# Attention 1 of a one-core vision tower: QKV from unnormalised rows, score row 7 summed on TensorE, a third value buffer for GpSimd, and an order of the value stage written out by hand

## The reference, cut to what matters

```
h = h + _L1_attn_ref(_layernorm(h, axis=-1), L1_attn_Wqkv, L1_attn_Wout)
h = h + _L1_ffn_ref(_layernorm(h, axis=-1), L1_ffn_base_W, ...)

def _layernorm(x, axis=-1, eps=1e-05):
    m = mean(x);  v = var(x);  return (x - m) / sqrt(v + eps)

def _L1_attn_ref(x, Wqkv, Wout):           # 16 heads of 16 channels, causal over the tiles
    q, k, v = split(x @ Wqkv.T)
    scores = clip(q . k / sqrt(16), -10, 10) + causal mask
    return (softmax(scores) @ v) @ Wout.T
```

## Time and profile before

| | us |
|---|---|
| median of 3 runs | 787.02 (785.82 to 787.16) |
| the profiled execution | 790.46 |
| its span in the trace | 788.6 |
| PE busy over the span | 701.5 |
| DVE busy | 499.5 |
| ACT busy | 391.7 |
| POOL busy | 420.2 |

### The profile page before, as it was taken

One profiled execution on the slowest core, in us unless ns is written; L12 is line 12 of the kernel. 1 busy time (PEld: TensorE's weight loads), 2 busy tenths in 40 slices (PEclk: granted clock), 3 DMA queues, 4 the chain that ended last, 5 costly groups with the idle time before them and its releaser, 6 DMA issues.

```text
span 788.6 us, 13036 instructions
## 1 busy us (share of the span) xinstructions
PE 701.5 (89%) x4209; PEld 600.4 (76%) x4209; DVE 499.5 (63%) x1182; ACT 391.7 (50%) x998; POOL 420.2 (53%) x358
## 2 busy tenths in 40 slices
PE   3999999999999999999829718999999999778788
PEld 3889998988989887654628618999999999435776
DVE  3678887777877787769989661322322232388966
ACT  4576675766757565533134433444444444147261
POOL 5767867768586760458869022334333432126860
PEclk9999999999999999999869957999999999779799
DMA  7955233432443030000030069899989993210001
GB/s 227 264 145 166 65 115 111 118 112 64 117 113 101 20 108 1 1 0 1 0 108 0 1 271 341 309 338 315 335 315 344 320 316 126 74 75 0 1 2 66
DMA packets 47085, 108.58 MB, mean 138 GB/s; under 512 B 5049, under 2 KB 24749, under 8 KB 39597
## 3 DMA queue, kind: packets, MB, share of 16 engines
q1 hardware_dynamic: 44428, 100.68, 38.4%
q0 software_dynamic: 2592, 7.10, 2.5%
HBM read 101.58 MB, written 6.17 MB: 137 GB/s over the span
## 4 chain that ended last, share of the span: by engine, by line
PE 72%; DVE 13%; POOL 4%; SPq 4%; ACT 3%; DMA 2%; issue 2%; DVEq 0%; ACTq 0%; POOLq 0%
PE banks L1808 12%; PE banks L1816 12%; PE banks L292 9%; PE banks L294 8%; PE banks L293 8%; PE banks L299 5%; PE banks L305 4%; PE banks L1348 3%; DVE a_o L1694 2%; DVE a_prod L1226 2%; SPq L386 2%; PE banks L1322 1%; PE banks L2159 1%; PE banks L1382 1%; POOL a_prod L1201 1%
## 5 line engine op out<-in xcount | busy, mean ns | idle before, releaser
L420 POOL TENSOR_TENSOR x_lo<-xraw,x_hi 128x512 fp32r<-128x512 f32 x81 | 106.3, 1312 | 77.8 <-ACT x_hi L414 77.7
L1898 ACT ACTIVATE hid<-banks,b 128x128 f32<-128x128 f32 x216 | 79.3, 367 | 110.4 <-PE banks L1808 107.8
L292 PE MATMUL banks<-wc_hi,x_hi 128*128 128x256 f32 x324 | 97.1, 300 | 13.3 <-POOL x_hi L423 9.8
L2065 DVE TENSOR_TENSOR res<-banks,xb 128x256 f32<-128x256 f32 x27 | 11.5, 424 | 127.9 <-PE banks L1816 127.9
L294 PE MATMUL banks<-wc_hi,x_lo 128*128 128x256 f32 x324 | 92.1, 284 | 0.0
L293 PE MATMUL banks<-wc_lo,x_hi 128*128 128x256 f32 x324 | 92.0, 284 | 0.0
L1936 POOL TENSOR_TENSOR y<-bve,mhalf 128x1 f32<-128x1 f32 x27 | 20.4, 755 | 105.6 <-DVE bve L2073 105.6
L456 DVE BATCH_NORM_STATS2 stats<-banks 128x6 f32<-128x256 f32 x81 | 34.6, 427 | 65.0 <-ACT pe_sb L450 64.3
L292 PEld LDWEIGHTS banks<-wc_hi,x_hi 128*128 128x128 f32 x324 | 62.1, 192 | 15.6 <-issue 10.0
L1808 PEld LDWEIGHTS banks<-xT,w_raw 128*128 128x128 f32 x448 | 68.0, 196 | 5.8 <-ACT xT L1886 0.9
L414 ACT ACTIVATE x_hi<-xraw 128x768 fp32r<-128x768 f32 (+1 forms) x81 | 66.6, 830 | 10.2 <-DMA xraw<-in_x_rest 10.2
(11 more groups left out here) (342 smaller groups left out, 1845.4 us busy)
## 6 DMA issues: line engine op xcount, KB each, us to landing
w_raw<-in_w SPq DMA_DIRECT2D x28, 1024.0 KB
xraw<-in_x_main SPq DMA_DIRECT2D x26, 768.0 KB
w1more<-in_w SPq DMA_DIRECT2D x13, 1024.0 KB
w2more<-in_w SPq DMA_DIRECT2D x13, 1024.0 KB
xraw<-in_x_rest SPq DMA_DIRECT2D x48, 96.0 KB
xraw<-in_x_rest SPq DMA_DIRECT2D x26, 114.0 KB
yl<-y_rows SPq DMA_DIRECT2D x2, 1028.0 KB, 6.9
a_w<-in_qkv_w SPq DMA_DIRECT2D x2, 768.0 KB, 5.4
```

The source lines that it names most:

```text
L292: pe.matmul(dst, a[0], b[0], start=start, stop=False)
L420: pool.tensor_tensor(x_lo[:, i % RING_X, :], xraw[:, k, 0:KF].rearrange("p c b -> p (c b)"), x_hi[:, i % RING_X, 0:KF * P], ALU.subtract). ...
L1898: act.activation(hid[:, s % 2, fc, :], bank(fc % 2, 0, P), ACT.Gelu, bias=b1[:, bass.ds(e * FC + fc, 1)]).then_inc(sem("gelu_made"), 1)
```

## The change

Six things change, all in attention 1 and around it.

1. The rows are not normalised before QKV. While the first experts' rows are gathered, PE sums the columns of `a_w[1]` with four matmuls against a matrix of ones, and DVE takes the column means off the weights (`center_qkv`, four operations). PE turns h itself, as soon as the pair of tiles is combined. The inverse deviation is applied when ACT copies q, k and v out of PSUM (`copy_scaled_qkv`). The ten normalisations on ACT and the three shifts on DVE go. Of rows that DVE reads as queries in PSUM (4, 6, 9) ACT scales the query in place, one more operation each.
2. Score rows: POOL makes the products of rows 1, 3, 5, 7, 8 (9 before, now DVE's). PE sums the products of row 7 by 16 matmuls; DVE only clips them. The first half of the softmax stands before DVE's last rows.
3. POOL has three slots for value products instead of two (the third is the buffer `yl`), and folds from four keys on instead of six, so rows 3 and 4 are folded too.
4. The order of PE and ACT in the value stage is written out call by call. The output products wait for all scores from row 0 on, not from row 2 on.
5. ACT measures rows 0 to 4 with two operations each (the mean comes out of the first one); DVE measures 5 to 9, and adds rows 7 and 8 to h before it waits for ACT's measurements.
6. The groups of z use the banks 2, 2, 3 instead of 2, 3, 2.

```diff
-        ON_ACT = 7
+        ON_ACT = 5
@@
-            jobs = [("row", t + 1, t == 6 if layer == 0 else t % 2 == 1)]
+            jobs = [("row", t + 1, t == 6 if layer == 0 else t in POOL_ROWS)]
...
+        POOL_ROWS = (1, 3, 5, 7, 8)
+        SUMMED_ROWS = {7: 6}
@@ def kept_keys
-            return (n + 1) // 2 if n > HALF else n
+            return (n + 1) // 2 if n > (HALF if layer == 0 else 3) else n
@@ def pool_slot
-            return a_prod[:, 2 + POOL_VALUES[layer].index(t) % 2, :]
+            i = POOL_VALUES[layer].index(t)
+            if layer == 1 and i % 3 == 2:
+                return yl[:, :, :].rearrange("p q c -> p (q c)")[:, 0:T * C]
+            return a_prod[:, 2 + i % (2 + layer), :]
@@
+        def pe_sum_row(pe, t):
+
+            n, i = t + 1, [job[0] for job in pool_jobs(1)].index(t)
+            pe.wait_ge(sem("a_pool_prod_made"), len(pool_jobs(0)) + i + 1)
+            by_channel = job_slot(1, i)[:, 0:n * C].rearrange("p (x d) -> p x d", d=D16)
+            for ch in range(D16):
+                last = pe.matmul(bank(SUMMED_ROWS[t], 0, n * H16), ident[:, :], by_channel[:, :, ch],
+                                 start=(ch == 0), stop=(ch == D16 - 1))
+            last.then_inc(sem("a_summed"), 1)
@@ def turn_x
-            pe.wait_ge(sem("a_xn_made"), seen(layer, "xn_made", t + 1))
+            if layer == 0:
+                pe.wait_ge(sem("a_xn_made"), t + 1)
+            else:
+                pe.wait_ge(sem("y_added"), 4 * (t // 2 + 1))
...
-            turn(pe, bank(t % 2), a_xn[:, t % 2, :]).then_inc(sem("a_turned"), 1)
+            turn(pe, bank(t % 2), a_xn[:, t % 2, :] if layer == 0 else h_at(t)).then_inc(sem("a_turned"), 1)
@@ def project_o
-                if layer == 1 and t == 2:
+                if layer == 1 and t == 0:
                     pe.wait_ge(sem("a_s_made"), seen(1, "s_made", T))
@@
+        def copy_scaled_qkv(act, t):
+            inverse = rstd[0][:, t:t + 1]
+            for part in range(3):
+                if t == batch_of("attention 1", part)[1]:
+                    act.wait_ge(sem("rstd_made"), batch_of("attention 1", part)[0] + 1)
+            act.wait_ge(sem("a_qkv_done"), seen(1, "qkv_done", 2 * t + 1))
+            a = 0
+            if t in queries_in_bank(1):
+                act.activation(qk_bank(t, 0, C), qk_bank(t, 0, C), ACT.Identity, scale=inverse)
+                a = C
+            act.activation(a_qkv[:, t, a:2 * C], qk_bank(t, a, 2 * C), ACT.Identity, scale=inverse).then_inc(sem("a_qkv_made"), 1)
...
@@ def dve_attention
-                for t in range(T + 1):
-                    if t < T:
-                        row_scores(dve, link, 1, t)
-                    if t == T - 2:
-                        softmax_half(dve, link, 1, 0)
+                for t in range(0, 8, 2):
+                    row_scores(dve, link, 1, t)
                     if t:
                         pool_sums(dve, link, 1, t - 1)
+                softmax_half(dve, link, 1, 0)
+                row_scores(dve, link, 1, T - 1)
+                pool_sums(dve, link, 1, T - 2)
...
+                    clip(dve, link, 1, "row", t, t + 1)
                 softmax_half(dve, link, 1, 1)
@@ end of the value stage on DVE
+                add_rows(dve, 8)
+                row_variances(dve, 2 * T + 2 * ON_ACT, ON_ACT)
                 for t in range(ON_ACT, T):
-                    add_rows(dve, t)
-                    dve.wait_ge(sem("a_h_made"), seen(1, "h_made", t + 1))
+                    if t == 7:
+                        add_rows(dve, 9)
+                    dve.wait_ge(sem("a_h_made"), seen(1, "h_made", T if t >= 7 else 9))
                     tile_stats(dve, "low rank", t, h_at(t))
-                    if t == ON_ACT:
-                        row_variances(dve, 2 * T + 3 * ON_ACT, ON_ACT)
...
-        ADDED = {5: ((0, 1), (2,)), 7: ((3,), (4,)), 9: ((5,), (6,))}
+        ADDED = {5: ((0, 1), (2,)), 7: ((3,), (4,)), 9: ((5,), (6, 7))}
@@
+        def center_qkv(dve):
+
+            dve.wait_ge(sem("route_summed"), 3)
+            for c in range(CH):
+                for means, a, b in ((bank(3, 0, 2 * C), 0, 2 * C), (bank(5), 2 * C, QKV)):
+                    dve.scalar_tensor_tensor(out=a_w[1][:, c, a:b], in0=means, scalar=-1.0 / C, in1=a_w[1][:, c, a:b],
+                                             op0=ALU.mult, op1=ALU.add)
```

149 lines of the change are left out of this document (93 added, 56 removed).

## The result

The changed kernel takes **780.6 us** (median of 4 runs, 778.46 to 781.80) against 787.09 (4 runs, 785.82 to 792.79) for the kernel before, measured beside it. The ratio is 0.9895 (95% interval 0.9863 to 0.9927), 8.3 us faster (5.7 to 10.8). Forecast were 776.8 us and −10.2. The profiled executions took 780.92 and 790.46; their spans are 779.1 and 788.6, 9.5 apart.

The account below looks back on a forecast made before the run. TensorE was taken as the main bound (72% of the chain, VectorE 13%), waiting on VectorE and GpSimd. Terms −5.8 −4.2 −1.1 = −11.1, with 0.9 given back −10.2 from 787.02: 776.8 us, range 774.3 to 781.3.

Parts of the forecast that it names:

- turn of row 8: TensorE's turn of row 8 in the values starts at 750.3 instead of 756.09: −5.8 us.
- base product: TensorE's 40 passes after the values run at 2.4 GHz, 8.7 us instead of 9.8: −1.1.
- hand-overs given back: Hand-overs between engines in tail and values, few of them counted in the timetable: 0.9 us taken off the gain.
- The start: QKV start: TensorE turns h without waiting for normalised rows, so QKV ends at 723.3, 4.0 us earlier.
- Row 7's sum: Scores: TensorE sums row 7 in 16 matmuls, 6.2 us from 723.3 to 729.6, hidden behind VectorE's rows.
- The third slot and the folds cancel: Values on GpSimd: slot waits removed against two new folds of 1.27; 22.55 us instead of 22.43, end at 750.0.
- Values on TensorE: Output products, z and turns: 10.3 us of work from row 3's output product, ending at 750.3, just behind GpSimd.
- The tail: From turn of row 8 to base product: VectorE's 4.03 us wait for ScalarE goes, 8.6 instead of 12.8: −4.2.
- it doesn't do what it says: Rival: another wait in the tail covers the removed one, only the start is gained: 781; chance 0.09 shared with blocked order.
- The clock: Rival: TensorE's clock falls before the values: 778.7, or 779.8 if it also falls in the tail; chance 0.2.
- Slower: Rival: QKV stays at 1.2 GHz, 2.1 us more per tile, up to 797 in all; chance 0.05.
- blocked: Rival: TensorE's written value order waits for VectorE's rows 5 and 7: 780 to 782; chance 0.09 shared with no tail gain.

Follow-up runs that it names:

- again: The changed kernel once more, without an edit, in five rounds beside the kernel before: 779.31 us, ratio 0.9897.
- oldorder: The changed kernel with TensorE's and ScalarE's values in the loop order of the kernel before; slots, folds, row 7's sum, five measured rows kept: 782.61 us, ratio 0.9921.
- row7dve: The changed kernel with score row 7 summed on VectorE again and no TensorE matmuls for it: 782.55 us, ratio 0.9906.
- wait7: The changed kernel with ScalarE measuring rows 5 and 6 too, and VectorE waiting for them before adding rows 8 and 9: 785.92 us, ratio 0.9964.

## Why the prediction held, and where it was off

The direction, the places and the range (774.3 to 781.3) held; the size was too large, −10.2 against −8.3 in the medians and −9.5 in the traces. Term by term, with the mean of the kernel before's two traces and that of the changed kernel's two and the one without centring, all from the combine on:

| term | forecast | measured |
|---|---|---|
| turn of row 8 | −5.8 | 66.56 to 61.23: −5.3 |
| of it, up to tile 1 of QKV | −4.0 | 12.04 to 7.89: −4.2 |
| of it, tile 1 to turn 8 | −1.8 | 54.52 to 53.33: −1.2 |
| turn 8 to base product | −4.2 | 12.77 to 9.64: −3.1 |
| base product | −1.1 | 9.76 to 8.64: −1.1 |
| rest | 0 | 10.01 to 10.11: +0.1 |
| hand-overs given back | +0.9 | in the terms above |
| sum | −10.2 | −9.5 |

- **The start.** First turn forecast at 691.5, seen at 691.19 (the combine stood 0.38 earlier in this trace); tile 1 at 697.5 and 697.30; first value on GpSimd at 727.45 and 726.68; last clip at 733.3, ended at 732.58. Right, and it went through whole.
- **Row 7's sum** was put at 6.2 and took 7.1 (32 passes from 722.38). That was a slip of arithmetic, not of the rows: 64 passes of 104 columns in the mean took 11.56, so 32 of 128 take 11.56 · 32/64 · 128/104 = 7.1. This cost nothing: VectorE has no idle time from 705.81 to 731.95, and the clips hang on its own work.
- **GpSimd.** Forecast 22.55 from first product to last fold, measured 22.83; folds 1.27 and 1.28, as priced. The prediction's own terms give less than it wrote (22.43 − 2.7 + 2 · 1.27 = 22.3), and the 0.5 on top is a wait for a slot that it had at nothing: 0.53 ahead of row 3, and none in `again`. "The third slot and the folds cancel" was right for GpSimd. But a fold is not an equal of a wait, since TensorE's turns grow without it: the slot brings 1.2 at the end, the folds next to nothing. The Trainium skill's "GPSIMD Engine Reference", section "Engine selection", advises against two-input elementwise work on GpSimd; here two folds there cost nothing at the end (0.2 us gained), because they shorten TensorE's turns by 1.7 in exchange (1.95 to 1.05 and 2.39 to 1.58).
- **Values on TensorE**, the first step that was mis-sized: forecast to reach turn 8 0.3 behind the last fold, it came 1.1 behind. The work counted (10.3 from the product of row 3) was right, the waits were not: 11.5 passed from 739.11 to 750.65, so 1.2 of waits where 0.9 was put. And the start of that work is GpSimd's: the turn of row 4 waits for its second new fold (1.25, and 0.49 in `again`), which the timetable had at nothing.
- **The tail**, the second and larger one: forecast 8.6 from turn 8 to base, measured 9.64. By the prediction's own price list the work there is 7.3 (the turn of row 8 2.23, two output products 1.74, five z 2.2, five turns 1.1), so waits took 2.4, not 1.1. Each round of turn, copy and next product leaves TensorE 0.25 to 0.56 idle where nothing else stands between. The 0.9 given back covered part of it. The reason given was right only in half as well: the prediction books the −4.2 to the wait that goes, and `oldorder` has no such wait and still takes 12.50. Its rival "it doesn't do what it says", in which the removed wait is covered by another in the same place, is what the old order shows in the tail (2.19 for row 9's output product); the new order keeps it from coming true.
- **The clock**, a rival with 0.2. It didn't fall. But its price was wrong as well: in `row7dve` it fell at this very place and the end stayed, while in the tail the fall cost 1.8 (`wait7`), where the rival had 1.1. The sentence of the Trainium skill's "TensorE: Matmul & The Clock Gate" ("What's actually happening"), that the slow level is the default and activity lifts it, agrees with both; the conclusion that every new wait on TensorE is a danger doesn't: it is one only where TensorE's work is what comes last.
- **Slower, blocked, or not what it says:** none of it in the kernel as it was written. The order's danger was real in a small size: it costs 0.8 ahead of turn 8 and gives 2.9 behind. The gated rows, forecast with 0.5 us to spare, are ready with none: VectorE's last operation on them ends at 769.09, as the base product does, and TensorE doesn't wait for it.
- **The number itself.** 776.8 was 787.02 − 10.2, and 787.02 was the median of three runs. In larger sets of the same kernel on three chips the median was 788.9 to 791.1, and spans vary by some 3 us with where the combine starts, ahead of nearly all that is changed. The profiled execution's 790.46 was the better base: less 9.5 it is 781.0, and 780.92 was measured. The prediction knew the gap of 3.4 between the two and carried its difference over to the lower one; it was the three runs that were low. Nor is a profiled execution slower as a rule, as was said ahead of the prediction: in eleven of the twelve experiments it lies below its kernel's median (778.63 against 779.31 in `again`).

What stays open: the traces give 9.5, the ratios 8.3 and 8.1 (`again`) with intervals that hold both, and the plain medians of that second set, 789.13 and 779.31, lie 9.8 apart. Which is nearest can't be told.
